# Slot products of 52 rows on half of TensorE each, with another front end, in a two-layer adapter and expert kernel

## The reference

```python
y    = x @ W.T + b + 2 * (x @ A[slot]) @ B[slot]            # 512 -> 512, adapter rank 16
base = y @ W_base.T + b_base
w    = softmax over the top 2 of (y @ W_router.T)           # 8 experts
lora = 2 * einsum('ter,te,eor->to', y @ A_experts, w, B_experts)   # rank 16 per expert
out  = x + base + lora
```

## Time and profile before

| | |
|---|---|
| median of 3 runs | 67.6 us (67.44 to 67.7) |
| profiled execution | 67.57 us, span 65.8 us |
| TensorE busy / weight loads | 94% / 92% of the span |
| VectorE, ScalarE, GpSimd | 55%, 33%, 26% |
| granted TensorE clock | 1.00 in all stretches |
| DMA | 10.55 MB, mean 160 GB/s |

### The profile page before, as it was taken

The page is one execution under the profiler, slowest core; times in us unless marked ns, Lnnn a source line. Parts: engine busy times, 40 slices in busy tenths (PEclk is TensorE's granted clock), DMA queues, the critical chain, the costliest instruction groups (busy, mean ns, idle before and its releaser), DMA issues.

```text
span 65.8 us, 1181 instructions
## 1 busy us (share of the span) xinstructions
PE 61.9 (94%) x424; PEld 60.8 (92%) x424; DVE 35.9 (55%) x103; ACT 21.5 (33%) x46; POOL 17.0 (26%) x30
## 2 busy tenths in 40 slices
PE   5999979999999999999999999999999999999930
PEld 5979879999999999998999999999999999999920
DVE  0056289998599667015935495002668363857320
ACT  0660358905989399127104100010201040020000
POOL 6810000000699982695390000010100000000000
PEclk9999999999999999999999999999999999999999
DMA  0899998219999004245559999700044000013532
GB/s 0 247 376 259 393 411 262 71 54 175 217 356 369 25 0 101 60 104 129 123 136 339 275 283 401 267 15 0 0 159 159 10 0 0 0 66 123 215 146 87
DMA packets 5865, 10.55 MB, mean 160 GB/s; under 512 B 731, under 2 KB 2523, under 8 KB 5860
## 3 DMA queue, kind: packets, MB, share of 16 engines
q1 hardware_dynamic: 5570, 10.15, 48.0%
q10 hardware_dynamic: 290, 0.33, 1.5%
HBM read 7.37 MB, written 2.10 MB: 144 GB/s over the span
## 4 chain that ended last, share of the span: by engine, by line
PE 83%; DMA 9%; SPq 1%; ACT 1%; DVE 1%; issue 1%
PE ps L661 26%; PE ps L673 19%; PE ps L567 17%; DMA wt<-w_chunks 9%; PE ps L721 9%; PE ps L628 5%; PE ps L696 2%; PE ps L701 2%; PE ps L684 1%; PE ps L707 1%; SPq L223 1%; ACT wt_hi L330 1%; PE ps L639 1%; DVE xn L520 1%
## 5 line engine op out<-in xcount | busy, mean ns | idle before, releaser
L661 PE MATMUL ps<-am,x_hi 128*128 128x384 f32 x64 | 16.6, 340 | 0.0
L673 PE MATMUL ps<-bm,x_hi 128*128 128x280 f32 x64 | 13.0, 297 | 0.0
L661 PEld LDWEIGHTS ps<-am,x_hi 128*128 128x128 f32 x64 | 11.4, 188 | 0.0
L661 PE MATMUL ps<-am,x_lo 128*128 128x384 f32 x32 | 10.8, 338 | 0.0
L297 POOL TENSOR_TENSOR x_lo<-xt,x_hi 128x512 fp32r<-128x512 f32 x8 | 10.8, 1367 | 0.0
L673 PEld LDWEIGHTS ps<-bm,x_hi 128*128 128x128 f32 x64 | 10.2, 188 | 0.0
L673 PE MATMUL ps<-bm,x_lo 128*128 128x280 f32 x32 | 9.3, 291 | 0.0
L567 PE MATMUL ps<-wt_hi 128*128 128x280 f32 (+1 forms) x32 | 7.4, 327 | 0.5 <-ACT wt_hi L330 0.3
L520 DVE TENSOR_TENSOR xn<-ps,xn 128x280 f32<-128x280 f32 (+1 forms) x16 | 6.1, 418 | 2.4 <-PE ps L721 2.3
L567 PE MATMUL ps<-wt_lo,wt_hi 128*128 128x280 f32 (+1 forms) x32 | 7.0, 316 | 0.0
L567 PE MATMUL ps<-wt_hi,wt_lo 128*128 128x280 f32 (+1 forms) x32 | 6.5, 310 | 0.0
(11 more groups left out here) (70 smaller groups left out, 98.5 us busy)
## 6 DMA issues: line engine op xcount, KB each, us to landing
xt<-x_t SPq DMA_DIRECT2D x4, 512.0 KB, 6.5
xn<-x_n SPq DMA_DIRECT2D x4, 512.0 KB, 6.0
out_n<-xn SPq DMA_DIRECT2D x7, 256.0 KB, 2.0
wt<-w_chunks SPq DMA_DIRECT2D x3, 582.0 KB, 6.6
g_st<-g_hl SPq DMA_DIRECT2D x12, 81.0 KB, 2.1
ab<-adapters SPq DMA_DIRECT2D x8, 64.0 KB, 2.7
wt<-w_chunks SPq DMA_DIRECT2D x2, 128.0 KB, 2.9
btt<-b_t SPq DMA_DIRECT2D x1, 256.0 KB, 5.0
```

The lines of the kernel that those rows point to most:

```text
L661: last = mm(a_bank(b)[:, 0:R + WA], v[:, p, i, tok], am[:, i, level, at:at + R + WA], start=(i == 0 and n == 0), stop=False, skip_group_ch ...
L673: mm(b_bank(b)[:, 0:QB], v[:, p, i, tok], bm[:, i, level, :], start=(i == 0 and n == 0), stop=False, skip_group_check=True)
```

## The change

- **Slot products of 52 rows.** A block's operands are its own 16 hi, 16 lo and 16 hi rows and 4 constants (two of `b_base`, two of b C). The even block's lie in partitions 0 to 51, the odd one's in 64 to 115 (`HP` = 64); the two matmuls of a pair are built for half of the array's rows each (64 x 128, at row 0 and at row 64) and write different banks. One transpose gives 116 rows. VectorE's `split` is two instructions of 16 rows.
- **G's rows** go out in 24 transfers of 16 rows (six a pair), the constants in 8 of one row for all pairs; the four of `b_base` are issued before G is there, and so are the tokens of pairs 0 and 1.
- **Front end.** Weight block 1 comes in two transfers, the C columns first. `b_base` goes to a buffer of its own, behind blocks 2 and 3 in SyncE's queue; ScalarE rounds it between weight blocks 1 and 2, VectorE makes its rest. All slot numbers are read at once, before x of pair 0. The first bias product is ScalarE's. The sum of 128 rows is folded to 64, and its hi and lo fill one tile of 128 rows, so the bias product has 2 matmuls. GpSimd's split of A waits for that tile. x of pairs 2 and 3 is rounded in one instruction each.
- **Order.** `slots_routed(0)` comes after `routed(3)`; `weighted_transpose(0)` after `plain(1)`; `plain(2)` before the experts of blocks 0 and 1; `stack(1)`, `split(1)` and ScalarE's `stack_t(1)` move accordingly.

The core of the diff:

```diff
@@ -52,9 +52,11 @@
 WA = NT + QA
 COLS = [slice(0, QB), slice(QB, WC)]
 W0_PIECES = [slice(D // 2, D), slice(0, D // 2), slice(D, D + QB), slice(D + QB, CB)]
-HSTEP = P + R
-LROW, HROW, CROW = 2 * R, 4 * R, 6 * R
-GK = CROW + 2
+HP = P // 2
+HSTEP = P + HP
+LROW, HROW, CROW = R, 2 * R, 3 * R
+SK = CROW + 4
+GK = HP + SK
 AW = R + WA + R
...
         g_st = sb("g_st", [P, PAIRS, WC], F32R)
         bsum = sb("bsum", [P, WC])
-        bsum_hl = sb("bsum_hl", [P, 2, WC], F32R)
-
-        h_stack = sb("h_stack", [P, PAIRS, 2 * HSTEP])
+        bsum_st = sb("bsum_st", [P, WC], F32R)
+        cb_hl = sb("cb_hl", [HP + 1, 2, WC], F32R)
+        c_hl, bb_hl = cb_hl[0:1], cb_hl[HP:HP + 1]
...
@@ -221,16 +236,16 @@
 
             for n in (0, 1):
                 sp.dma_start(wt[:, 0, W0_PIECES[n]], w[:, 0, W0_PIECES[n]]).then_inc(w0_in[n], 16)
-            for k in range(1, KB):
+            sp.dma_start(wt[:, 1, D:CB], w[:, 1, D:CB]).then_inc(w_in[1], 16)
+            sp.dma_start(wt[:, 1, 0:D], w[:, 1, 0:D]).then_inc(w1_rest_in, 16)
+            for k in range(2, KB):
                 sp.dma_start(wt[:, k, :], w[:, k, :]).then_inc(w_in[k], 16)
-                if k == 1:
-                    sp.wait_ge(bsum_zero, 1)
-                    sp.dma_start(bsum[0:1, :], bbase).then_inc(bbase_in, 16)
+            sp.dma_start(bb, bbase).then_inc(bbase_in, 16)
+            sp.wait_ge(idx_in, 16)
+            _, slots = nc.values_load_multi_w_load_instructions(
+                idx_sb[0:1, :], engines=[mybir.EngineType.SP], min_val=0, max_val=SLOTS - 1)
             sp.dma_start(xt[:, 0], x[:, 0]).then_inc(x_in[0], 16)
-
-            sp.wait_ge(idx_in, 16)
-            for b in range(NB):
-                slot = sp.value_load(idx_sb[0:1, b:b + 1], min_val=0, max_val=SLOTS - 1)
+            for b, slot in enumerate(slots):
                 sp.dma_start(ab[:, b].rearrange("p c k r -> p (c k r)"),
                              tbl[bass.ds(slot, 1)].rearrange("s p n -> (s p) n")).then_inc(ab_in, 16)
...
@@ -238,29 +253,46 @@
             for p in range(2, PAIRS):
                 sp.dma_start(xt[:, p], x[:, p]).then_inc(x_in[p], 16)
 
+            def adapter_rows(row, p, part):
+                for t in range(2):
+                    src = (2 * p + t) * R
+                    sp.dma_start(g_st[t * HP + row:t * HP + row + R, p, :].bitcast(F32),
+                                 g_hl[src:src + R, part, :].bitcast(F32)).then_inc(gst_in[p], 16)
+
+            def spread(row, src):
+                for t in range(2):
+                    at = t * HP + row
+                    sp.dma_start(g_st[at:at + 1, :, :].bitcast(F32),
+                                 src.bitcast(F32).to_broadcast([1, PAIRS, WC])).then_inc(cst_in, 16)
+
+            def tokens(p):
+                sp.dma_start(xn[:, 2 * p:2 * p + 2, :],
+                             xn_in[2 * p:2 * p + 2].rearrange("b p c -> p b c")).then_inc(xn_in_done[p], 16)
+
+            tokens(0)
+            tokens(1)
+
+            sp.wait_ge(bb_hi_done, 1)
+            spread(CROW, bb_hl[:, 0:1, :])
+            sp.wait_ge(bb_lo_done, 1)
+            spread(CROW + 1, bb_hl[:, 1:2, :])
+
             for p in range(PAIRS):
-                rows = slice(2 * R * p, 2 * R * (p + 1))
                 if p == 0:
                     sp.wait_ge(g_hi_done, 2)
-                sp.dma_start(g_st[0:LROW, p, :].bitcast(F32),
-                             g_hl[rows, 0, :].bitcast(F32)).then_inc(gst_in[p], 16)
-                sp.dma_start(g_st[HROW:CROW, p, :].bitcast(F32),
-                             g_hl[rows, 0, :].bitcast(F32)).then_inc(gst_in[p], 16)
+                adapter_rows(0, p, 0)
+                adapter_rows(HROW, p, 0)
                 if p == 0:
                     sp.wait_ge(g_lo_done, 2)
-                sp.dma_start(g_st[LROW:HROW, p, :].bitcast(F32),
-                             g_hl[rows, 1, :].bitcast(F32)).then_inc(gst_in[p], 16)
+                adapter_rows(LROW, p, 1)
                 if p == 0:
 
                     sp.wait_ge(c_hi_done, 2)
                     sp.wait_ge(c_lo_done, 2)
                     for i in range(2):
-                        sp.dma_start(g_st[CROW + i:CROW + i + 1, :, :].bitcast(F32),
-                                     bsum_hl[0:1, i:i + 1, :].bitcast(F32).to_broadcast([1, PAIRS, WC])
-                                     ).then_inc(cst_in, 16)
-            for p in range(PAIRS):
-                sp.dma_start(xn[:, 2 * p:2 * p + 2, :],
-                             xn_in[2 * p:2 * p + 2].rearrange("b p c -> p b c")).then_inc(xn_in_done[p], 16)
+                        spread(CROW + 2 + i, c_hl[:, i:i + 1, :])
+            tokens(2)
+            tokens(3)
 
             for b in range(NB - 2):
...
@@ -338,6 +370,9 @@
                 hi(wt_hi[:, 0, c], wt[:, 0, c]).then_inc(w0_hi_done, 1)
             act.wait_ge(w0_in[3], 16)
             hi(wt_hi[:, 0, D + QB:CH], wt[:, 0, D + QB:CH]).then_inc(wc_hi_done, 1)
+            act.wait_ge(w0_in[2], 16)
+            nc.scalar.activation(bsum[:], wt[:, 0, D:CH], ACT.Copy,
+                                 scale=wt[:, 0, CH:CH + 1]).then_inc(bsum_first, 1)
 
...
@@ -347,19 +382,21 @@
 
             def x_high(p):
                 act.wait_ge(x_in[p], 16)
-                for k in range(0, KB, 2):
-                    hi(x_hi[:, p, k:k + 2, :], xt[:, p, k:k + 2, :]).then_inc(x_hi_done, 1)
+                step = 2 if p < 2 else KB
+                for k in range(0, KB, step):
+                    hi(x_hi[:, p, k:k + step, :], xt[:, p, k:k + step, :]).then_inc(x_hi_done, 1)
 
             w_high(1)
+            act.wait_ge(bbase_in, 16)
+            hi(bb_hl[:, 0], bb).then_inc(bb_hi_done, 1)
             w_high(2)
             w_high(3)
             x_high(0)
             act.wait_ge(ab_in, 16 * NB)
             hi(bs_hi[:].rearrange("p k b r -> p b k r"), ab[:, :, 1]).then_inc(ab_hi_done, 1)
             hi(as_hl[:, :, :, 0, :], ab[:, :, 0]).then_inc(ab_hi_done, 1)
-            act.wait_ge(bsum_done, KB)
-            hi(bsum_hl[:, 0], bsum[:]).then_inc(bsum_hi_done, 1)
-
+            act.wait_ge(halves_done, 1)
+            hi(bsum_st[0:HP], bsum[0:HP]).then_inc(bsum_hi_done, 1)
             for i in range(KB):
...
@@ -389,7 +426,13 @@
                 act.wait_ge(hwt_ps, p + 1)
                 hi(hw_hi[:, 2 * p:2 * p + 2, :], a_scratch(p)).then_inc(hw_hi_done, 1)
 
-            for p in range(PAIRS):
+            stack_t(0)
+            shares(0)
+            stack_t(1)
+            weighted_hi(0)
+            shares(1)
+            weighted_hi(1)
+            for p in range(2, PAIRS):
                 stack_t(p)
                 shares(p)
...
+                    bias_sum(k - 1)
+                else:
+                    dve.wait_ge(bb_hi_done, 1)
+                    lo(bb_hl[:, 1], bb, bb_hl[:, 0]).then_inc(bb_lo_done, 1)
             bias_sum(KB - 1)
+            dve.wait_ge(bsum_done, KB - 1)
+            nc.vector.tensor_copy(upper, bsum[HP:P]).then_inc(upper_done, 1)
+            dve.wait_ge(upper_done, 1)
+            nc.vector.tensor_tensor(bsum[0:HP], bsum[0:HP], upper, ALU.add).then_inc(halves_done, 1)
             dve.wait_ge(ab_hi_done, 1)
             lo(bs_lo[:].rearrange("p k b r -> p b k r"), ab[:, :, 1],
                bs_hi[:].rearrange("p k b r -> p b k r")).then_inc(bs_lo_done, 1)
+            dve.wait_ge(bsum_hi_done, 1)
+            lo(bsum_st[HP:P], bsum[0:HP], bsum_st[0:HP]).then_inc(bsum_lo_done, 1)
 
             for i in range(KB):
-                if i == 2:
-                    dve.wait_ge(bsum_hi_done, 1)
-                    lo(bsum_hl[:, 1], bsum[:], bsum_hl[:, 0]).then_inc(bsum_lo_done, 1)
                 dve.wait_ge(m_hi_done, 2 * i + 1)
...
@@ -635,9 +687,7 @@
             pe.wait_ge(bsum_lo_done, 1)
             pe.wait_ge(m_lo_done, 4)
             for s, c in enumerate(COLS):
-                for i in range(2):
-                    last = mm(ps[:, C_BANK + s, 0:c.stop - c.start], ones_r[:], bsum_hl[:, i, c],
-                              start=(i == 0), stop=(i == 1))
+                last = mm(ps[:, C_BANK + s, 0:c.stop - c.start], ones_r[:], bsum_st[:, c], start=True, stop=True)
             last.then_inc(c_done, 1)
...
@@ -681,24 +731,26 @@
                     pe.wait_ge(c_lo_done, 2)
                 pe.wait_ge(stack_done, p + 1)
                 for t in range(2):
-                    last = mm(b_bank(2 * p + t)[0:GK, T0:], h_stack[:, p, t * P:t * P + GK], ident[:],
+                    last = mm(b_bank(2 * p + t)[0:GK, T0:], h_stack[:, (2 * p + t) * P:(2 * p + t) * P + GK], ident[:],
                               is_transpose=True, start=True, stop=True, skip_group_check=True)
                 last.then_inc(ht_ps, 1)
 
             def slots_routed(p):
 
                 if p == 0:
-                    pe.wait_ge(cst_in, 32)
-                pe.wait_ge(ht_lo_done, p + 1)
-                pe.wait_ge(gst_in[p], 48)
+                    pe.wait_ge(cst_in, 128)
```

(48 more changed lines are left out.)

26 lines of the change are left out of this document (13 added, 13 removed).

## The result

| | before | changed |
|---|---|---|
| median of 4 runs | 67.54 us (67.44 to 67.7) | 70.59 us (70.17 to 70.99) |
| profiled execution | 67.57, span 65.8 | 70.99, span 69.2 |
| ratio, 95% interval | | 1.048, 1.043 to 1.054 |
| TensorE busy / weight loads | 94% / 92% | 92% / 87% |
| granted TensorE clock | 1.00 | 1.00 |

The change is slower by 3.05 us where 0.2 less was forecast, outside the range. The clock is not part of it.

The account below looks back on a forecast made before the run. After the second weight block's load, TensorE alone was taken to bound the kernel until the last add. Terms +0.47 - 0.30 - 0.17 - 0.20 = -0.20 took 67.57 to 67.4 us, range 66.5 to 69.5.

Parts of the forecast that it names:

- Step 7: Slot products of 52 rows on half tiles: 0.84 us gained, 0.64 lost over eight visits, -0.20 us in all.
- Rival C: TensorE runs empty at each of 16 tile changes, 2.6 us in place of 0.64: 69.4 us; chance 0.17.
- Step 6: G's rows in 24 transfers, constants in 8: rows land at 32.3, just covered when TensorE needs them; no time change.
- Step 3: Bias sum folded to 64 rows on VectorE's queue before G: G starts at 19.85 instead of 19.38, +0.47 us.
- Step 2: b_base queued behind blocks 2 and 3: lands at 9.0, ScalarE ends block 2 before TensorE wants it; nothing lost.
- Step 1: Weight block 1 in two transfers: TensorE's 0.33 us idle before 8.62 goes, but the bias fold takes that gain back.
- step 5: First routed slot pair moved behind block 3's routed product: 0.51 becomes 0.34, -0.17 us.
- Step 4: Bias product on TensorE with 2 matmuls instead of 4: -0.30 us, half of 0.60, all on the path.
- Rival B: The two slot matmuls of a pair do not overlap, so 0.84 is missing: 68.2 us; chance 0.13.
- rival A: The change of tile costs nothing, -0.64 more: 66.7 us, with the full gain 66.5; chance 0.25.
- Rival D: b_base lands at 10.6, TensorE stalls 0.8 before block 2, G begins near 21.4, +1.5: 68.9 us; chance 0.12.

Follow-up runs that it names:

- the doubled pairs: Changed kernel with each slot pair issued twice in a row, alternating even and odd half, no visit more: 71.65 us, ratio 1.058.
- the run without the fold: Kernel before with only weight block 1 in two transfers and the later order of the first slot products: 67.08 us, ratio 0.995.

## Why the prediction was wrong

- **Step 7, the cost of a change to half tiles**, failed, and it is the term that decided. The gain was of the right kind, and at its upper end: seven pairs lose their second matmul whole, 3 x 0.13 + 4 x 0.17 = 1.07 (taken as 0.84). The cost was taken as 0.04 a change, from the transposes' 0.08 a visit; measured are 0.19 a change and 0.38 a visit, 3.0 us for eight in place of 0.64. The term is +2.0 instead of -0.20 (2.2 by the two traces), two thirds of the 3.25 us between forecast and median. The transposes were a poor neighbour: they use the whole array, and their weights are loaded 0.10 to 0.13 ahead. The other end, 0.16, was reckoned from matmul against matmul and left out the weights, whose load then starts only with its matmul; that this makes the difference from 0.16 to 0.19 is my reading of the loads, and no run separates it.
- **Rival C** was the right mechanism, with a chance of 0.17. Its price, 2.6 for the 16 changes, is 0.4 short of the 3.0 measured; its 69.4 is 1.2 short of the median, and the rest of that is front and transfers. The Trainium skill (TensorEngine Tiling (Array Packing), "Key Properties") has a mode change drain TensorE; the trace agrees, by the loads at 43.13 and 43.45, and it puts the price at 0.19 us a change. The same skill (TensorE: Matmul & The Clock Gate, "The mechanism") has loads overlap between row groups; the trace agrees, by the 0.18 for two loads and by the doubled pairs. Both rules held, and 0.33 was too high a chance for a forecast that went against the first.
- **Step 6, transfers**, had the price of an issue right: 16 rows take 0.59 and stand 0.63 apart, like 32. "Just covered" was too hopeful: in the profiled execution the last issue for the second pair takes 1.24 us, its rows land 3.20 after it starts instead of 2.1, and TensorE waits 0.80. What it is worth in the medians is not settled: the run with block 2's plain product ahead of the pair gained nothing that could be told.
- **Step 3, the fold**, was right in its pieces and 0.28 short in sum (G at 20.13, foretold 19.85): 0.24 of it is there when VectorE is through with the bias sums, at 16.04 against 15.8. (The step's own figures, 15.8 + 0.55 + 0.83, make 17.2 and not its 17.3.) The first routed product came at 24.07, not 23.7; another 0.08 went as G's first matmul, coming out of a wait, took 0.21 to the next instead of 0.13. **Step 2** was right in the landing of this execution (9.05, taken as 9.0), which is partly luck, since it varied from 8.80 to 10.17 between profiled executions, and wrong in "nothing lost": it followed TensorE's need of block 2, and not VectorE's, which stood 1.37 idle.
- **Step 1** was right (no idle at block 1), and it and step 5 together show as a gain only in the run without the fold. **Step 4** was right: 0.30. **Step 5** was right for the first pair, whose wait of 0.17 is gone.
- **Rival B** fell by the doubled pairs and **rival A** by every chain. **Rival D** did not happen in the changed kernel's two profiled executions (b_base landed at 9.05 and 9.04), but its mechanism is real: in the run with whole tiles where the row landed at 10.17, TensorE waited 0.55 before block 2, where 0.8 was foretold.

## What to carry to other kernels

Two small matmuls on halves of the array pay only if enough of them stand together: here a visit costs 0.38 us and a second matmul of a pair saves 0.13 to 0.17, so by these figures, an estimate that no run here tested, three pairs or more must share a visit. Before costing work at nothing because its consumer has time, follow its queue: what else stands behind it on the same engine. And where a step stands in a queue decides what it costs: ahead of G the folded bias and b_base put off the first routed product by 0.5 us, while in idle time the fold left M's first piece where it was (17.61) and halved the bias product.
